# A transformer's second stage in another order: the loop body begins at another place, on all five engines

## The reference

```python
for i in range(DEPTH):
    x = attn_layer(shift_tokens(x), Wqkv[i], q_scale[i], k_scale[i], Wo[i]) + x
    x = ffn_layer(shift_tokens(x), ln_g[i], ln_b[i], W1[i], b1[i], W2[i], b2[i]) + x
```

```python
q = l2norm(q) * qs
k = l2norm(k) * ksc
q = q * cos * scale + rotate_half(q) * sin * scale
k = k * cos * inv + rotate_half(k) * sin * inv
out = local_attention(q, k, v).transpose(0, 2, 1, 3).reshape(b, n, INNER) @ Wo
```

## Time and profile before

| what | value |
|---|---|
| this execution, its span | 4903.19 us, 4901.4 us |
| TensorE busy, passes | 4101.4 us (84%), 60260 |
| TensorE weight loads | 2147.2 us (44%) |
| VectorE busy | 4055.3 us (83%) |
| GpSimd busy | 3517.2 us (72%) |
| ScalarE busy | 2979.9 us (61%) |
| chain that ended last | PE 61%, issue 4%, SP's queue 2%, others 1% or less each |
| instruction packets (queue q8) | 488, 8.00 MB |

### The profile page before, as it was taken

One profiled execution on the slowest core, in us unless ns is written; L12 is line 12 of the kernel. 1 busy time (PEld: TensorE's weight loads), 2 busy tenths in 40 slices (PEclk: granted clock), 3 DMA queues, 4 the chain that ended last, 5 costly groups with the idle time before them and its releaser, 6 DMA issues.

```text
span 4901.4 us, 154523 instructions
## 1 busy us (share of the span) xinstructions
PE 4101.4 (84%) x60260; PEld 2147.2 (44%) x60260; DVE 4055.3 (83%) x7132; ACT 2979.9 (61%) x4240; POOL 3517.2 (72%) x1655
## 2 busy tenths in 40 slices
PE   3666666666656999999998999899998999899997
PEld 1232233233223555555554555455554555455554
DVE  6999999999955888888887888788887888788885
ACT  5999999999963554455544554454454445444552
POOL 4999899999975766667666666666666666666663
PEclk9655555555558999999999999999999999999999
DMA  0000000000004544445444544454444444444444
GB/s 14 3 5 9 6 9 5 5 9 5 3 7 102 121 110 104 107 116 118 107 100 106 116 111 100 104 118 110 99 105 118 106 100 105 120 108 97 110 111 107
DMA packets 230497, 381.82 MB, mean 78 GB/s; under 512 B 38112, under 2 KB 59232, under 8 KB 229728
## 3 DMA queue, kind: packets, MB, share of 16 engines
q1 hardware_dynamic: 229856, 372.57, 32.3%
HBM read 51.57 MB, written 18.61 MB: 14 GB/s over the span
## 4 chain that ended last, share of the span: by engine, by line
PE 61%; issue 4%; SPq 2%; DVE 1%; ACT 1%; DMA 1%; POOL 0%; DVEq 0%; POOLq 0%; ACTq 0%
PE pb L1348 15%; PE pb L1404 8%; PE pb L1355 7%; PE pb L1430 7%; PE pb L1420 7%; PE pb L1371 5%; PE pb L1445 5%; PE pb L1470 3%; PE pb L1383 3%; ACT v L1620 1%; PE pb L1436 1%; SPq L1227 1%; PE pb L1441 1%; DMA xs<-hist 1%; DVE tab L1844 0%
## 5 line engine op out<-in xcount | busy, mean ns | idle before, releaser
L734 POOL TENSOR_TENSOR W<-W 128x1280 f32<-128x1280 f32 x416 | 955.0, 2319 | 141.6 <-ACT W L585 139.8
L585 ACT ACTIVATE W<-S,lam 128x512 f32<-128x512 f32 (+3 forms) x2048 | 951.9, 553 | 84.4 <-DVE lam L878 73.0
L1749 POOL TENSOR_TENSOR m<-m 128x1024 f32<-128x1024 f32 x384 | 902.8, 2363 | 67.8 <-DVE m L1857 67.6
L849 DVE BATCH_NORM_STATS2 stats<-W 128x6 f32<-128x512 f32 (+3 forms) x2048 | 832.4, 478 | 58.1 <-POOL W L734 56.9
L1755 POOL TENSOR_TENSOR sm<-sm,mx 128x1024 f32<-128x1024 f32 x192 | 451.7, 2353 | 512.5 <-DVE mx L1871 512.5
L1348 PE MATMUL pb<-xs,wg 128*128 128x512 f32 x1536 | 765.7, 634 | 47.5 <-DMA xs<-hist 33.2
L1602 ACT ACTIVATE lnn<-pb,cst 128x1024 f32<-128x1024 f32 x192 | 213.9, 1114 | 804.5 <-PE pb L1355 804.5
L1880 DVE SCALAR_TENSOR_TENSOR nf<-rn,m 128x1024 f32<-128x1024 f32 x384 | 616.6, 1637 | 90.7 <-ACT rn L1611 75.8
L1597 ACT ACTIVATE sq<-pb 128x1024 f32<-128x1024 f32 x384 | 381.9, 1021 | 496.1 <-PE pb L1348 496.1
L1745 POOL TENSOR_TENSOR sqs<-sq 128x1024 f32<-128x1024 f32 x192 | 456.9, 2380 | 221.7 <-ACT sq L1597 221.7
L1760 POOL TENSOR_TENSOR pr<-pr,rsum 128x1024 f32<-128x1024 f32 x192 | 407.5, 2122 | 288.8 <-DVE rsum L1893 288.6
(11 more groups left out here) (123 smaller groups left out, 7111.2 us busy)
## 6 DMA issues: line engine op xcount, KB each, us to landing
qkn<-nf SPq DMA_DIRECT2D x1536, 128.0 KB, 2.4
vr<-v SPq DMA_DIRECT2D x96, 768.0 KB, 5.9
vr<-v SPq DMA_DIRECT2D x96, 192.0 KB, 5.5
xr<-hist SPq DMA_DIRECT2D x48, 256.0 KB, 2.9
hist<-xo SPq DMA_DIRECT2D x47, 256.0 KB, 3.8
wg<-wqkv SPq DMA_DIRECT2D x24, 384.0 KB, 3.8
xs<-hist SPq DMA_DIRECT2D x48, 128.0 KB
vr<-v SPq DMA_DIRECT2D x96, 64.0 KB, 6.2
```

The source lines that it names most:

```text
L585: ins = nc.scalar.activation(W[:, p, h, c], S[:, j % 2, h, c], ACT.Abs_reciprocal_sqrt, bias=lam[:, j, i:i + 1])
L734: nc.gpsimd.tensor_tensor(W[:, p, h, :], W[:, p, h, :], W[:, p, h, :], ALU.mult).then_inc(s_wp[p], 1)
L849: ins = nc.vector.bn_stats(out=stats[:, p, h * NBLK + u, :], in_=W[:, p, h, UOFF[u]:UOFF[u] + UNIT[u]])
L1749: nc.gpsimd.tensor_tensor(m1[:, which, :, :], m1[:, which, :, :], m2[:, which, ::-1, :], ALU.add)\
```

## The change

The order of `body` changes on all engines, and with it `HOLD` (banks and order). TensorE's body now begins with the last part of the attention of piece b - 2 (weigh3), where it began with its variance; it ends with q2. The waits of the parts move out of them into functions `..._due` that the body calls, so that they can stand apart from the matmuls: three times a `take` or a wait now stands in front of a run of small matmuls and its own matmuls behind it. `Y_BANK` is computed.

```diff
-        Y_BANK = (0, 1, 4, 5)
...
-            ("var", 2, 3), ("turn0", 1, 0), ("v3", 1, 2), ("weigh0", 1, 4), ("norm3", 1, 0), ("gate1", 2, 7),
...
+            ("weigh3", 2, 2), ("k2", 1, 6), ("wo", 2, 2), ("score1", 1, 6), ("norm2", 1, 0), ("mean", 2, 5),
...
+        HELD_LAST = {c: max((back, i) for i, (name, back, _) in enumerate(HOLD) if c in banks(name)) for c in range(8)}
+        Y_BANK = [c for c in range(8) if HELD_LAST[c] < (HOLD[PLACE["var"]][1], PLACE["var"])]
```

By this rule `Y_BANK` is [4]. On the sync queue (SP):

```diff
                     load_projections(b, l, k == 0, (0, 1))
+                if live(b, 1):
+                    rotated(b - 1, 2)
+                if live(b, 0):
+                    load_projections(b, l, k == 0, (2, 3))
+                if live(b, 1):
+                    load_xr(b - 1)
-                if live(b, 3):
+                if live(b, 3) and not is_body(b, END + 3):
                     store(b - 3)
-                if live(b, 2):
-                    load_w2(b - 2, l, k == 2)
-                if live(b, 1):
-                    rotated(b - 1, 2)
-                if live(b, 0):
-                    load_projections(b, l, k == 0, (2, 3))
...
                 if live(b, 1):
+                    load_w1(b - 1, l, k == 1)
+                if live(b, 0):
+                    rolled(b, 0)
+                if live(b, 1):
+                    load_w2(b - 1, l, k == 1)
+                if live(b, 1):
                     load_vectors(b - 1, l, k == 1)
-                if live(b, 0):
-                    load_xr(b)
-                if live(b, 0):
-                    rolled(b, 0)
-                if live(b, 1):
-                    load_w1(b - 1, l, k == 1)
```

On TensorE, two of the waits' functions and two of the three places:

```diff
+            def due(s, value):
+                pe.wait_ge(s, value)
+                pe.sem_inc(held["pe"], 1)
...
+            def squares_due(n, g):
+                due(s_sqs, at(n, g))
...
             def norms(n, g, out):
-                pe.wait_ge(s_sqs, at(n, g))
-                pe.sem_inc(held["pe"], 1)
...
+                if live(b, 1):
+                    take("norm2", b)
+                    squares_due(b - 1, 2)
+                if live(b, 1):
+                    take("score1", b)
+                    rotated_due(b - 1, 1)
+                    scores(b - 1, 1, 0, bank("score1"))
+                if live(b, 1):
+                    norms(b - 1, 2, bank("norm2"))
...
+                if live(b, 2):
+                    take("up1", b)
+                if live(b, 1):
+                    take("score2", b)
+                    rotated_due(b - 1, 2)
+                    scores(b - 1, 2, 0, bank("score2"))
                 if live(b, 1):
                     scores(b - 1, 2, 1, bank("score2"))
-                if live(b, 0):
-                    project(b, 0, 0, take("q0", b))
-                if live(b, 0):
-                    project(b, 0, 1, take("k0", b))
                 if live(b, 2):
-                    ups(b - 2, 1, take("up1", b))
+                    ups(b - 2, 1, bank("up1"))
```

VectorE takes the second `finish` of a group and the masks earlier, and the maximum of group 2 last; `residual` gets a wait for `finished` of the piece before:

```diff
                 if live(b, 0):
                     weighted(b, 0)
                 if live(b, 0):
-                    finish(b, 3, 1)
-                if live(b, 0):
-                    inverse_denominators(b, 1)
-                if live(b, 0):
                     mask(b, 2)
                 if live(b, 0):
-                    row_max(b, 2)
+                    finish(b, 3, 0)
                 if live(b, 0):
-                    finish(b, 3, 0)
+                    finish(b, 3, 1)
                 if live(b, 1):
                     gate(b - 1, 2)
+                if live(b, 0):
+                    row_max(b, 2)
...
             def residual(n):
+                dve.wait_ge(s_xo, at(n - 1, 0, 1))
+                dve.sem_inc(held["dve"], 1)
```

354 lines of the change are left out of this document (200 added, 154 removed), and 10 rows, old and new, of the table HOLD.

## The result

The change makes the kernel slower: 5021.51 us, the median of 4 runs (5007.35 to 5025.82), against 4908.75 us for the kernel before beside it (4 runs), a ratio of 1.0228, interval 1.0202 to 1.0255. The forecast was 4811, range to 4915. The profiled execution took 5017.24 us, 114 more than that of before.

The account below looks back on a forecast made before the run. The prediction took TensorE to set the pace, with idle time and a lower clock to lose. Its terms, -44 - 31 - 53 + 18 + 13 + 5 = -92, took 4903 to 4811 us, range 4767 to 4915.

Parts of the forecast that it names:

- Page wait: TensorE's stop inside weigh3 for a late instruction page, 57.0 us, mostly goes with weigh3 first in the body: -44 us.
- I take 0.3 us a step to stay: Page wait assumed left after the change, at the loop's head and the page at 256: 13 of 57 us.
- rival 3: Two instruction pages in a row late at the branch, 2.7 us a step: 4946 us, slower from 1.8; chance 0.15.
- Clock: Half-clock stretches behind weigh3's stop go with the stop: 17 steps at 1.8 us, -31 us.
- Small gaps: TensorE's idle behind small passes at L1348, L1420 and L1445 goes, covered by large matmuls: -53 us.
- Waits on the chain: TensorE's matmuls queued behind hoisted waits, such as score2 and score1, cost nothing unless VectorE is late.
- The tightest chain is to norm0: From score2 over group 2's mask, finishes and k0's rotation to norm0, which waits about 0.4 us, 0 to 1.1.
- Other engines: Changed orders on ScalarE, GpSimd and VectorE make norm0, norm3 and gate0 wait 0.3 us a step: +13 us.
- Rival 2: VectorE takes over at norm0, norm3 and gate0, costing 75 us instead of 13: 4873 us; chance 0.10.
- New gaps: TensorE idles at q3 behind score1, gate0 behind weigh0 and norm3 behind turn0, 0.4 us a step together: +18 us.
- End: Last transposes at the kernel's end alternate with VectorE's additions, since only one bank is left for them: +5 us.
- Rivals 1 to 3: 1: page wait only moves, 4886 us, chance 0.12; 2: VectorE takes over, 4873, 0.10; 3: two late pages, 4946, 0.15.

Follow-up runs that it names:

- b_hoist: The kernel before with q0's waits put ahead of score2 and those of out ahead of score0's first half: 4919.20 us, ratio 1.003.
- b_chain3: The kernel before with three more DMA moves, into an unread buffer, ahead of group 0's eight, TensorE's instructions unchanged: 4986.07 us, ratio 1.016.
- b_weigh2: The kernel before with weigh2's second half moved behind score0's first half: 5069.31 us, ratio 1.0315.
- a_half: The changed kernel with four of group 0's eight DMA moves left out: 4970.56 us, ratio 1.0128 to the kernel before.

## Why the prediction was wrong

The bottleneck, TensorE, and the rise of its idle time as the thing to sum over were right. By the terms of the sum, each over the same 47 steps:

- **Page wait: -44 forecast, +12 measured** (59.1 to 71.3). The step that failed is "I take 0.3 us a step to stay". It took 1.5. The two reasons given for the lower end, that the stream stands still at the head for turn3's copy and that score0's second half is queued early, did not hold: the branch waits 2.36 us for the page. The mechanism was rival 3's, two pages in a row, at 1.5 us a step instead of its 2.7, and so below its own limit of 1.8. By itself it would have made the kernel no slower: 4811 and the 56 us missed here are 4867.
- **Clock: -31 forecast, about -37 measured, in part by luck.** The stretches at 0.50 went from 75 to 48 us in ordinary steps (18 steps to 7) and from 64 to 17 us at the boundaries. At half of their length, as the 1.8 us for a stretch of 3.4 have it, that is 14 us for the ordinary steps, all that the forecast spoke of, and 23 for the boundaries, which it didn't. Busy time still rose by 11, since the runs of small passes got 47 us longer: scores 292.5 to 320.1, weighing 646.8 to 666.5 in the groups of instructions. Three more of them a step now start behind a larger matmul or a wait, at some 0.15 us each, 21 us; the rest of the 47 I can't name. The 47 were not in the sum.
- **Small gaps: -53 forecast, -53 measured in the list, 13 gained.** v0's and up0's, 17.4 and 22.6, lay between k0 and score0, where the chain sets the end, and came back as waits on it. Only q0's 12.9 was time to be had. b_hoist shows it from the other side: a gap can vanish and nothing be gained.
- **Waits on the chain: 0 forecast, +110 measured** (72.3 on the moves, 34.0 on sm, 3.2 on the gate). This is the step that made the sign: "The tightest chain is to norm0". The part on the other engines priced that one alone and put waits on all others at nothing. It never priced that of group 0, from k0 over the eight moves to score0, and left out that up1 and half of weigh2 were moved from inside it. The earlier trace rows has L1371's wait on the moves only at boundaries, and I read this as slack. It was 0.4 us from the landing to score0's start. b_chain3, b_weigh2 and a_half show this chain at work. It isn't all of the 110: score3, moved 3.6 us ahead, waits 21.4 of them for group 3's moves, and the 34.0 are for group 3's mask. They lie in the same stretch, so group 0's chain would have filled them anyway, but a_half shows that shortening it gives back 51 and no more.
- **Other engines: +13 forecast, 48 measured**, of it norm3 14.5 and weigh0 33.3. Norm0, the one worked out, waits no more than it did (16.7, before 22.9). Rival 2's mechanism, at other places.
- **New gaps: +18 forecast, +5 measured** (L1414 +8.8, L1477's 15.1 against 19.1).
- **End: +5 forecast, +11 measured**: the serial blocks as priced, the late load not.
- **At 0 in the forecast:** the start of stage 2, +8 (its cause wasn't looked for), and the boundaries, -35 in all five, as the waits there for xs (16.3), the moves (13.1) and VectorE (6.2 less) went.

The measured terms add up to 117, against 114, when clock and small runs together are taken as the 11 us by which busy time rose. Rivals 1 to 3 had a part of it each, and none had the chain. (By the forecast's own rule its chances come to 0.74 faster and 0.15 slower, not 0.73 and 0.16.) What would have told of it was in the timeline of before: the landing of the last move beside score0's start.

## What to carry to other kernels

Before work is moved, measure how long after its last input each waiting instruction really starts; a wait that never shows in a list may have 0.4 us of slack, and work taken out of the stretch in front of it is then paid in full. When a program is longer than one page of instructions, treat where the borders fall as part of the schedule: find them by counting, look at packets and waits around each, and try a few placements of the loop's head before changing any order, since an order compared at one placement is compared with its borders. Gaps count as gain only if the next wait down the stream has slack.
